# Deep attention layers on one core: q left unscaled, the softmax exponential in 64-key pieces from PSUM, and the feed-forward's next-block front moved ahead

## The reference, cut to what matters

```python
for i in range(DEPTH):                       # DEPTH = 6, HEADS = 16, DIM_HEAD = 64, WINDOW = 32
    x = attn_layer(shift_tokens(x), Wqkv[i], q_scale[i], k_scale[i], Wo[i]) + x
    x = ffn_layer(shift_tokens(x), ln_g[i], ln_b[i], W1[i], b1[i], W2[i], b2[i]) + x

def attn_layer(x, Wqkv, qs, ksc, Wo):
    q, k, v = split(x @ Wqkv)                # 16 heads of 64
    q = l2norm(q) * qs;  k = l2norm(k) * ksc
    q = rotary(q, scale);  k = rotary(k, 1 / scale)
    sim = q @ k^T * 8                        # each window of 32 queries sees its own and the last 32 keys
    out = softmax(where(mask, -max, sim)) @ v
    return out @ Wo

def ffn_layer(x, g, bln, W1, b1, W2, b2):
    xn = layernorm(x) * g + bln
    a, gate = split(xn @ W1 + b1)
    return a * gelu(gate) @ W2 + b2
```

## Time and profile before

| | |
|---|---|
| median of 3 runs | 6133.15 us (6132.75 to 6140.19) |
| the profiled execution: its own time | 6136.03 us |
| the profiled execution: its span | 6134.2 us |
| granted TensorE clock, mean | 0.866 of full speed |
| busy | PE 77%, DVE 70%, PE weight loads 60%, POOL 55%, ACT 46% |

### The profile page before, as it was taken

The page is one execution under the profiler, slowest core; times in us unless marked ns, Lnnn a source line. Parts: engine busy times, 40 slices in busy tenths (PEclk is TensorE's granted clock), DMA queues, the critical chain, the costliest instruction groups (busy, mean ns, idle before and its releaser), DMA issues. The chain is left out here.

```text
span 6134.2 us, 175865 instructions
## 1 busy us (share of the span) xinstructions
PE 4713.8 (77%) x70592; PEld 3658.9 (60%) x70592; DVE 4298.2 (70%) x6496; ACT 2838.3 (46%) x5349; POOL 3353.0 (55%) x1834
## 2 busy tenths in 40 slices
PE   4986999947887678885788866888668887678875
PEld 3664877745666456664566655666546665466664
DVE  4346999958886478873688836888358884588854
ACT  2552333315554355552455534555335554355542
POOL 0004666637775367762577725777347774367741
PEclk8897999968998789986899978999778997798887
DMA  1000000002222012220122211222102222022220
GB/s 29 0 0 19 1 0 0 0 32 57 54 54 65 4 45 54 54 62 20 38 57 56 56 28 31 54 54 54 41 18 54 54 54 55 7 52 53 54 60 22
DMA packets 151608, 229.83 MB, mean 37 GB/s; under 512 B 33038, under 2 KB 56460, under 8 KB 149900
## 3 DMA queue, kind: packets, MB, share of 16 engines
q1 hardware_dynamic: 150924, 219.36, 15.0%
HBM read 26.31 MB, written 4.19 MB: 5 GB/s over the span
## 5 line engine op out<-in xcount | busy, mean ns | idle before, releaser
L1993 POOL TENSOR_TENSOR spare<-raw,table 128x512 f32<-128x512 f32 x768 | 1318.7, 1743 | 296.5 <-ACT spare L1592 296.5
L2003 POOL TENSOR_TENSOR raw<-raw,rs 128x1024 f32<-128x1024 f32 x384 | 821.8, 2151 | 694.5 <-DVE rs L1782 694.5
L1761 DVE TENSOR_TENSOR raw<-raw,spare 128x1024 f32<-128x1024 f32 x384 | 795.8, 2072 | 13.2
L1754 DVE TENSOR_TENSOR raw<-raw,table 128x1024 f32<-128x1024 f32 x384 | 736.8, 1919 | 62.3 <-POOL spare L1993 57.8
L1400 PE MATMUL trn<-ident,E 128*128 128x128 f32 x1536 | 329.5, 353 | 475.2 <-POOL E L2031 353.7
L1804 DVE TENSOR_REDUCE mx<-sco 128x16 f32<-128x1024 f32 x192 | 235.1, 1225 | 533.9 <-PE sco L1385 533.8
L2031 POOL TENSOR_TENSOR E<-E,rden 128x1024 f32<-128x1024 f32 x192 | 447.3, 2330 | 258.2 <-DVE rden L1819 258.2
L1400 PEld LDWEIGHTS trn<-ident,E 128*128 128x128 f32 x1536 | 237.3, 182 | 550.2 <-issue 366.2
L1611 ACT ACTIVATE room<-trn 128x512 f32<-128x512 f32 x384 | 230.1, 599 | 580.5 <-PE trn L1400 580.1
L1366 PE MATMUL trn<-ident,raw 128*128 128x128 f32 x3072 | 484.7, 281 | 9.2 <-ACT kT L1600 3.8
L1748 DVE TENSOR_REDUCE ss<-spare 128x16 f32<-128x1024 f32 x384 | 464.1, 1209 | 16.5 <-ACT spare L1592 16.4
(11 more groups left out here) (220 smaller groups left out, 11388.7 us busy)
## 6 DMA issues: line engine op xcount, KB each, us to landing
Vw<-V SPq DMA_DIRECT2D x1344, 128.0 KB
Vw<-V SPq DMA_DIRECT2D x192, 64.0 KB
spare<-in_L_ffn_Wqkv SPq DMA_DIRECT2D x6, 1536.0 KB, 6.6
wo<-in_L_ffn_Wo SPq DMA_DIRECT2D x6, 512.0 KB, 3.9
X<-in_L_attn_x SPq DMA_DIRECT2D x16, 128.0 KB, 2.6
x_before_deep<-X SPq DMA_DIRECT2D x1, 2048.0 KB, 8.3
raw<-x_before_deep SPq DMA_DIRECT2D x1, 2048.0 KB, 8.0
out<-X SPq DMA_DIRECT2D x16, 128.0 KB, 2.0
```

The source lines that it names most:

```text
L1754: dve.tensor_tensor(x, x, table[:, part, 0, k][:, None, :].to_broadcast([P, H, HD]), ALU.mult).then_inc(cos_part, 1)
L1761: dve.tensor_tensor(x, x, t2[:, part], ALU.add).then_inc(summed, 1)
L1993: pool.tensor_tensor(dst[:, :, a], src[:, :, 1 - a], table[:, part, 1, k, 32 * a:32 * a + 32][:, None, :].to_broadcast([P, H, 32]), ALU.mu ...
L2003: pool.tensor_tensor(x, x, rs[:, at:at + H][:, :, None].to_broadcast([P, H, HD]), ALU.mult).then_inc(rotated, 1)
```

## The change

Attention: POOL scales k only (two instructions a sequence, steps 0 and 2). A DVE copy `keep_q` (step 13) keeps q's inverse norms as `rq`. `highest` writes the negated maxima, and a 128x16 product with `rq` gives `nb`; the subtraction of 128x1024 is gone. ACT makes each exponential straight from PSUM as exp(rq * score + nb), and since scale and bias are one value per partition, one instruction covers one head's 64 keys: 16 instructions for each half, 8 in one step and 8 in the next. PE turns q once it is summed, and the second use of `sco` waits for the exponentials where it waited for the subtraction.

Feed-forward: on each engine the next block's front stands about one third earlier; the last parts (`f_norm`, `f_affine`) stand at the end.

```diff
-SCALE_STEPS = (0, 2, 4, 6)
+SCALE_STEPS = (0, 2)
+KEEP_STEP = 13
...
# PE
-                pe.wait_ge(rotated, count(n * 4 + 2 * k + part + 1))
+                if part == 0:
+                    pe.wait_ge(summed, count(n * 4 + 2 * k + 1))
+                else:
+                    pe.wait_ge(rotated, count(n * 2 + k + 1))
...
-                    pe.wait_ge(lowered, count(N))
+                    pe.wait_ge(exped, count(N))
...
             def f_in(m):
+                pe.wait_ge(f_xnT, count(m))
                 pe.wait_ge(f_staged, count(m + 1))
...
+                if front:
+                    f_in(m + 1)
                 for t in range(3):
                     f_hidden(m, t)
-                    if front:
-                        (f_in, f_return, f_norm)[t](m + 1)
+                    if front and t == 0:
+                        f_return(m + 1)
                     if ahead:
                         for step in beside_feed(g, t):
                             prepare(l + 1, step)
+                if front:
+                    f_norm(m + 1)
                 f_output(m)
# ACT
-            def exps(n, o):
+            def exps(n, par, o, hp):
                 N = 2 * n + o
-                act.wait_ge(lowered, count(N + 1))
-                e = E[:, o].rearrange("p s j -> p (s j)")
-                act.activation(e, e, ACT.Exp).then_inc(exped, 1)
+                if hp == 0:
+                    act.wait_ge(biased, count(N + 1))
+                for s in range(ROWS // 2):
+                    j, k = divmod(s, 2)
+                    h = 8 * o + 2 * j + hp
+                    c = hp * (ROWS // 2) + s
+                    t = act.activation(E[:, o, 2 * s + hp], sco[:, hp, s * HD:(s + 1) * HD], ACT.Exp,
+                                       bias=nb[:, o, c:c + 1], scale=rq[:, par, k, h:h + 1])
+                if hp == 1:
+                    t.then_inc(exped, 1)
...
-                    if step == EXP_STEPS[o]:
-                        exps(n, o)
+                    if 0 <= step - EXP_STEPS[o] < 2:
+                        exps(n, par, o, step - EXP_STEPS[o])
...
+                if front:
+                    f_shift(m + 1)
                 for t in range(3):
                     f_gelus(m, t)
-                    if front and t == 0:
-                        f_shift(m + 1)
-                    if front and t == 2:
-                        f_affine(m + 1)
                     if ahead:
                         for step in beside_feed(g, t):
                             prepare(l + 1, step)
+                if front:
+                    f_affine(m + 1)
# DVE
+            def keep_q(n, par):
+
+                dve.wait_ge(inv_norm, count(n + 1))
+                dve.tensor_copy(rq[:, par], rs[:].rearrange("p (k a h) -> p k a h", k=2, a=2)[:, :, 0]).then_inc(q_scaled, 1)
...
-                dve.tensor_reduce(mx[:], s, AX.X, ALU.max).then_inc(maxed, 1)
+                dve.tensor_reduce(mx[:], s, AX.X, ALU.max, negate=True).then_inc(maxed, 1)
                 dve.wait_ge(maxed, count(N + 1))
...
-                dve.tensor_tensor(E[:, o].rearrange("p (s h) j -> p h s j", h=2), s,
-                                  m[:, :, :, None].to_broadcast([P, 2, ROWS // 2, HD]),
-                                  ALU.subtract).then_inc(lowered, 1)
+                dve.wait_ge(q_scaled, count(n + 1))
+                r = rq[:, par, :, 8 * o:8 * o + 8].rearrange("p k (j h) -> p h j k", h=2)
+                dve.tensor_tensor(nb[:, o].rearrange("p (h j k) -> p h j k", h=2, k=2),
+                                  mx[:].rearrange("p (h j k) -> p h j k", h=2, k=2), r,
+                                  ALU.mult).then_inc(biased, 1)
...
                     f_gated(m, t)
+                    if front and t == 0:
+                        f_stat(m + 1)
                     if front and t == 1:
-                        f_stat(m + 1)
-                    if front and t == 2:
                         f_normal(m + 1)
# SP, before the next layer's Wqkv is loaded
-                sp.wait_ge(rotated, count(l * NSEQ * 4))
+                sp.wait_ge(summed, count(l * NSEQ * 4))
```

More of the change, by code:

```diff
@@ L1147, in deep_stage @@
         mx = sb("mx", [P, ROWS])
+        rq = sb("rq", [P, 2, 2, H])
+        nb = sb("nb", [P, 2, ROWS])
         den = sb("den", [P, 2, ROWS])
@@ L1216, in deep_stage @@
         inv_norm = sem("inv_norm")
+        q_scaled = sem("q_scaled")
         cos_part = sem("cos_part")
@@ L1222, in deep_stage @@
         maxed = sem("maxed")
-        lowered = sem("lowered")
+        biased = sem("biased")
         exped = sem("exped")
@@ L1620, in drain_mix, with attend @@
                 act.activation(oT[:, r:r + 2, :].rearrange("p r t -> p (r t)"), acc[hp][:], ACT.Copy).then_inc(head_out, 1)
-            def attend(n, step):
+            def attend(n, par, step):
                 for o in range(2):
-                    if step == EXP_STEPS[o]:
-                        exps(n, o)
+                    if 0 <= step - EXP_STEPS[o] < 2:
+                        exps(n, par, o, step - EXP_STEPS[o])
                     if 0 <= step - FLIP_STEPS[o] < 2:
@@ L1646, in heads @@
                     if not first:
-                        attend(n - 1, h + STEPS)
-                    attend(n, h)
+                        attend(n - 1, 1 - par, h + STEPS)
+                    attend(n, par, h)
                     if ahead >= 2:
@@ L1673, in attention @@
                 for step in range(STEPS, LAST_STEP + 1):
-                    attend(n + NSEQ - 1, step)
+                    attend(n + NSEQ - 1, 1, step)
                 split_w1(l)
@@ L1771, in inverse @@
                 dve.wait_ge(newton, count(at + 2))
-                dve.wait_ge(rotated, count(n * 4))
+                dve.wait_ge(rotated, count(n * 2))
                 dve.tensor_tensor(rs[:].bitcast(I32), magic[:].bitcast(I32), seed[:].bitcast(I32),
@@ L1798, in project, with highest @@
                     inverse(n)
-            def highest(n, o, first):
+                if step == KEEP_STEP:
+                    keep_q(n, par)
+            def keep_q(n, par):
+                dve.wait_ge(inv_norm, count(n + 1))
+                dve.tensor_copy(rq[:, par], rs[:].rearrange("p (k a h) -> p k a h", k=2, a=2)[:, :, 0]).then_inc(q_scaled, 1)
+            def highest(n, par, o):
                 N = 2 * n + o
@@ L1803, in highest @@
                 s = sco[:].rearrange("p b (c j) -> p (b c) j", j=HD)
-                dve.tensor_reduce(mx[:], s, AX.X, ALU.max).then_inc(maxed, 1)
+                dve.tensor_reduce(mx[:], s, AX.X, ALU.max, negate=True).then_inc(maxed, 1)
                 dve.wait_ge(maxed, count(N + 1))
-                if not (first and o == 0):
-                    dve.wait_ge(p_turned, count(2 * N - 2))
-                s = sco[:].rearrange("p h (s j) -> p h s j", j=HD)
-                m = mx[:].rearrange("p (h s) -> p h s", h=2)
-                dve.tensor_tensor(E[:, o].rearrange("p (s h) j -> p h s j", h=2), s,
-                                  m[:, :, :, None].to_broadcast([P, 2, ROWS // 2, HD]),
-                                  ALU.subtract).then_inc(lowered, 1)
+                dve.wait_ge(q_scaled, count(n + 1))
[3 more added lines that the diff above has]
+                                  ALU.mult).then_inc(biased, 1)
             def totals(n, o):
@@ L1825, in add_attn, with attend @@
                                   ALU.add).then_inc(attn_added, 1)
-            def attend(n, step, l, s, first=False):
+            def attend(n, par, step, l, s):
                 for o in range(2):
                     if step == HIGHEST_STEPS[o]:
-                        highest(n, o, first)
+                        highest(n, par, o)
                     if step == TOTAL_STEPS[o]:
@@ L1840, in heads @@
                     if not first:
-                        attend(n - 1, h + STEPS, l, s - 1)
-                    attend(n, h, l, s, first)
+                        attend(n - 1, 1 - par, h + STEPS, l, s - 1)
+                    attend(n, par, h, l, s)
                     if ahead >= 2:
@@ L1886, in attention @@
                 for step in range(STEPS, LAST_STEP + 1):
-                    attend(n + NSEQ - 1, step, l, NSEQ - 1)
+                    attend(n + NSEQ - 1, 1, step, l, NSEQ - 1)
             def f_stat(m):
@@ L1995, in sine, with scale @@
                                        ALU.mult).then_inc(sin_part, 1)
-            def scale(n, par, k, part):
-                j = n * 4 + 2 * k + part
+            def scale(n, par, k):
                 pool.wait_ge(inv_norm, count(n + 1))
-                pool.wait_ge(summed, count(j + 1))
-                x = raw[:, par, k, part].rearrange("p (h d) -> p h d", d=HD)
-                at = (2 * k + part) * H
+                pool.wait_ge(summed, count(n * 4 + 2 * k + 2))
+                x = raw[:, par, k, 1].rearrange("p (h d) -> p h d", d=HD)
+                at = (2 * k + 1) * H
```

(5 more changed lines are left out.)

## The result

| | before | after |
|---|---|---|
| median | 6132.95 us (6125.1 to 6140.19, 4 runs) | 6601.36 us (6580.19 to 6623.1, 4 runs) |
| granted TensorE clock, mean | 0.866 | 0.847 |
| busy | PE 77%, DVE 70%, POOL 55%, ACT 46% | PE 75%, DVE 60%, POOL 42%, ACT 54% |

The change makes the kernel slower: ratio 1.0764 (95% interval 1.0726 to 1.0802). That is 468 us more, where the forecast had 124. Both shares that the change was to relieve, DVE and POOL, did fall; the time rose all the same.

A forecast was written before the change was run, and what follows sets the result against it. Bound: a loop of PE's turn and products, DVE from maximum to inverse norm, POOL's scale and normalise, with DVE close behind. 6136.0+302 (attention)-178 (feed-forward)=6260, or 6257 us by the median; own range 6200 to 6320, over all 6120 to 6385.

The forecast's parts named there:

- the feed-forward (-178): Feed-forward: earlier fronts save 31.6 us in each of five layers and 19.6 in the last, together 178 us less.
- The price of a piece (0.31): ACT in attention: each narrow 64-key exponential starts 0.31 us after the one before; sixteen a half take 4.96 us.
- rival (1): ACT's narrow exponentials cost 0.40 us each, 1632 of them on the chain: +147, so 6404 us; chance 0.10.
- rival (2): ACT's narrow exponentials cost 0.21 us each: -163, so 6094 us, faster than before; chance 0.21.
- The first half's row sum (T=10.25): DVE's row sum waits for ACT's exponentials and begins 10.25 us after the first-half maximum (T=0), 5.9 us later than before.
- DVE's arrival at the second maximum (22.1): DVE starts the second-half maximum 22.1 us after the first-half maximum, against 18.26 before: +3.85 us.
- Scores end near 20.3, before 22.1. DVE is now the later one.: PE finishes the second-half scores 20.3 us after the first-half maximum, before DVE is ready for its second maximum at 22.1.
- Rival (4): The exponentials' delay of ACT runs on into PE's projections; period 42 us for 40.55: +122, so 6379 us; chance 0.13.
- The second leg (-0.8): From second-half maximum to the next sequence's first: DVE's work from maximum to inverse norm shrinks by 0.8 us a period.
- 1 us short of being waited for: The second half's exponentials, 23.6 to about 29.6 us after the first maximum, lie beside the Newton iteration without delaying it.
- The layer's end (+7.7): End of each attention layer: later weight loading (about 4.6 us) and the very last half (+3.1) add 7.7 us together.
- 302 forecast: Attention: fourteen periods a layer add 42.7 us and the layer's end 7.7; 50.4 a layer, +302 us over six.

The follow-up runs named there:

- squares_first: The changed kernel with DVE's second sum of squares moved ahead of the first half's row sum (REDUCE step -9 to -10): 6243.11 us, ratio 1.0181.
- ffn_only: The kernel before with only the feed-forward part of the change: 5965.35 us, ratio 0.9729.
- pe_loop4: squares_first with TensorE's loop over the sequences holding four of them for two: 6212.56 us, ratio 1.0126.

## Why the prediction was wrong

- **Direction, and the feed-forward (-178).** Slower is right. The feed-forward gave 165 by itself; 30.5 us in layer 1 for 31.6, and 8.15 in the block costed for 8.7. Its mechanism held, and its size but for the last layer, where 12.3 us came for 19.6: 1.8 a block for 2.8.
- **The price of a piece (0.31).** It is 0.289, inside the bounds (0.21, 0.40). The upper bound was added up wrongly: 0.37 less 0.05 plus 0.10 is 0.42, and rival (1) would have stood at 6437. 1632 pieces at 0.021 less would have moved the sum by 34 us downward. Rival (1), dearer pieces, and rival (2), cheaper ones (0.21, faster below 0.234), are both ruled out. The estimate of 332 ns by the page's rule (the Trainium skill, "ScalarE: Activation LUTs", section "What ACT_TABLE_LOAD costs") is 0.043 us above the measurement.
- **The first half's row sum (T=10.25) and DVE's arrival at the second maximum (22.1).** 10.44 and 21.64. Both hold.
- **The step that failed: "Scores end near 20.3, before 22.1. DVE is now the later one."** They end at 25.6 (2644.39+0.45). I moved PE's wait for ACT by "about 2", from ACT's own extra work, and took ACT to wait for nobody else; it moved by 4.6, of which ACT's 2.26 us of waiting for DVE is the part that was left out. In `squares_first`, without that wait, it moved by 1.9, and the scores end at 20.0 (2480.96+0.45), as forecast. Of DVE's delayed queue I asked only what it does to DVE. I didn't ask who waits for its entries: ACT's squares go into a buffer that the sum of squares empties, and this sum had just been put 6 us later. The prediction named the cosine product and sum as queued behind the waiting row sum; the second sum of squares, queued there too, it didn't name, nor who waits for it. Its price is 358 us (`squares_first`), nearly the 341 by which the attention term was short. Rival (4), a delay of ACT that runs on into PE, had the right place but ACT's work for its cause, and so 122 us for its price.
- **TensorE's clock.** A term that the sum put at nothing without a reason. After 4.11 us of standing PE took 6.42 us from turn to turn for 3.57, so 2.9 of the 7.5 us from the turn to the second maximum.
- **The second leg (-0.8).** In layer 2 it averages 19.9 us over thirteen periods, and 19.4 before: +0.5. Where PE's loop turns, a stand of 3.6 us, mostly hidden before, comes out. I had costed the second half's pieces at nothing, "1 us short of being waited for"; they aren't waited for by DVE's row sum, but the turns of q and k behind them in ACT's queue are by PE.
- **The layer's end (+7.7).** 5.8 in layer 2.
- **The sum.** With the wait gone the attention costs 278 us over `ffn_only`, near the 302 forecast. That the two are so close is partly luck: the first leg is shorter than forecast (20.1 for 22.1) and the second longer (19.7 in layer 2's mean, for 40.55-22.1=18.45).

## What to carry to other kernels

When an instruction starts to wait, everything behind it in its queue is late, and each of those entries may be somebody's release: list for all of them, not just for the next ones, which buffer they free and who fills it. Small reductions that free a buffer belong ahead of a long wait; one number in a table was worth 5.4% here. Replacing one wide instruction by many narrow ones with per-row operands is paid on the engine that also frees other engines' buffers, so its whole time counts, and waits that hid something (a loop's turn, a lower clock) should be priced before they are moved.

## What the runs showed of the hardware

- ACT, in a run of narrow exponentials from PSUM: 0.289 us from start to start for 64 elements with two per-partition operands, 0.196 with one, 0.342 for 128 with two. That is 0.83 ns an element, 0.093 us for the second operand, and 0.05 us if the first costs the same (0.196-0.053-0.093). The copies of 512 without operands, 0.48 apart (2629.36 and the ones behind it), fit this: 0.05+0.43. I had expected 0.05 us of an operand to overlap in a run; of the second's 0.10 (0.37 against 0.27) 0.093 stays.
- TensorE stood 3.1 to 4.6 us where its loop turned (36 times each in the changed kernel and in `squares_first`, 18 times in `pe_loop4`), with no releaser in the profile. Four sequences in a body for two, three turns fewer in each of six layers, gave 31, 48 and 58 us where the stand was open, and 10 where it was covered; of the 31, most was in the last layer.
- After 4.11 us of standing, the granted clock was 0.52 over the next 7 us, in which PE was busy for 6.56; after 1.41 us of standing it was 1.00. After some 1.7 us both were seen: 1.00 in `squares_first` (1.75) and 0.57 in `pe_loop4` (1.69).
